# Summing two scattered halves in a fused decoder block: one half's loads ahead of the last tiles, additions on two engines, and a norm's short steps between them

## The chip, the cores and the metric

The kernel runs on one core of one Trainium2 chip. The metric is device time in microseconds (us) of one execution of the whole kernel, as a median of several runs. A profile is one execution taken by the hardware profiler; its clock starts at the start of the span, and all times of day below (such as 1405.73) are us on that clock. Engines: PE (TensorE), DVE (VectorE), ACT (ScalarE), POOL (GpSimd), SP (SyncE, which here only issues DMAs).

## The reference

A post-norm decoder block on 4 x 512 tokens of width 512, in float32: causal self-attention with 16 heads and rotary embedding, cross-attention over a masked context of 1601 rows, and a mixture of 16 experts (top 4 of each token) plus a shared expert. Only the end matters here:

```python
def step(acc, ws):
    wg, wu, wd, cw = ws
    return (acc + cw[:, None] * _swiglu_ffn(x, wg, wu, wd), None)
routed, _ = lax.scan(step, jnp.zeros_like(x), (w_gate, w_up, w_down, combine.T))
shared = _swiglu_ffn(x, sw_gate, sw_up, sw_down)
...
x = _layernorm(x + _L0_ffn_ref(x, ...), axis=-1)
```

Each token's result is its input plus the shared expert's output plus four weighted expert outputs, and of that sum a layer norm without scale or bias is taken.

## The kernel before

The 2048 tokens lie in SBUF as `rows`, 128 partitions x NT = 16 token tiles x D = 512. The routed experts (`routed_experts`) work on TILES = 79 slot tiles, numbered m = 0 to 78, each of 128 rows that belong to one expert. For each tile POOL gathers the rows by an indirect DMA (`gather`, L1881), PE turns and multiplies them with the expert's weights in three passes, ACT weighs the output into `y` (`weigh_y`, L1934), and POOL sends it out by an indirect DMA that adds each row to its token's row in DRAM (`scatter`, L1890). Two such accumulators exist, `acc[0]` and `acc[1]` (in the profile both are `acc_rows`): tile m adds to `acc[m % 2]`, and since two scatters to one tensor may not overlap, scatter m waits until scatter m - 2 has landed. `acc[0]` starts out as the input plus the shared expert. The semaphores `y_added[0]` and `y_added[1]` count the landings.

SP loads the experts' weights (L1860, 3 MB each); after the last of them it waits at L1873 until both accumulators are complete, that is until tiles 77 and 78 have landed.

Then `finish_rows` runs. The 16 token tiles are taken in five parts, `PARTS = ((0, 2), (2, 6), (6, 10), (10, 14), (14, 16))`, called part 0 to part 4 here. SP issues ten loads (L2086), for each part the even half into `rows` and the odd half into `odd_rows`; parts of four tiles are 1 MB a half, the others 0.5 MB. A part's semaphore `row_in[k]` reaches 32 when both halves are in. DVE then does, part by part: the additions `rows + odd_rows` (L2105), the statistics (L677), their aggregation (L684), and the short steps of `normalise`: `half_v` (L696), reciprocal (L699) of the square root which ACT has taken meanwhile (`root`, L690), two products (L702), `rstd` (L704), and the shift (L709). With `by_scalar=True` ACT scales the part's rows (L721). ACT's own order is for each part: sqrt, wait for the shift, scale; so the next part's sqrt stands behind this part's scaling. SP stores a part (L2091) when its rows are scaled. POOL has nothing to do in this stage. The program order of each engine is the order written in the code; there is no scheduler.

Of the kernel before, what the change touches and what calls it, by code (L numbers as in the profile page):

```python
# [28 lines left out]
ALU = mybir.AluOpType  # L29
# [8 lines left out]
EPS = 1e-5  # L38
# [3 lines left out]
NT = B * TT  # L42
# [13 lines left out]
TILES = (NT * P * TOPK + E * (SLOTS - 1)) // SLOTS  # L56
# [604 lines left out]
def layer_norm(nc, sem, ctx, rows, name, by_scalar=False, parts=tuple((b * TT, b * TT + TT) for b in range(B))):  # L661
# [9 lines left out]
    eps_set, gathered, aggregated = sem(name + "_eps_set"), sem(name + "_gathered"), sem(name + "_aggregated")  # L671
# [7 lines left out]
    def aggregate(dve, b):  # L679
        if b == 0:  # L680
            nc.vector.memset(eps[:, :], EPS).then_inc(eps_set, 1)
        for t in range(*parts[b]):
            dve.wait_ge(gathered, t + 1)
            nc.vector.bn_aggr(mean_var[:, t, :], stats[:, t, :]).then_inc(aggregated, 1)  # L684

    def root(act, b):
        mine = slice(*parts[b])
        act.wait_ge(eps_set, 1)
        act.wait_ge(aggregated, parts[b][1])
        nc.scalar.activation(rstd[:, mine], mean_var[:, mine, 1], ACT.Sqrt, bias=eps[:, 0:1]).then_inc(rooted, 1)  # L690

    def normalise(dve, b):

        mine = slice(*parts[b])
        dve.wait_ge(aggregated, parts[b][1])
# [1103 lines left out]
def routed_experts(nc, block, sem, w_split, x2_rows, acc, plan, done, ends):  # L1799
# [7 lines left out]
    with ExitStack() as ctx:  # L1807
# [31 lines left out]

        def added(m):  # L1840

            return y_added[m % 2], 16 * (m // 2 + 1)
# [11 lines left out]
        def _(sp):  # L1854
# [17 lines left out]
            for par in range(2):  # L1872
                sp.wait_ge(y_added[par], 16 * ((TILES + 1 - par) // 2))  # L1873

        @block.gpsimd
        def _(pool):
# [9 lines left out]
            def scatter(m):  # L1886
                if m >= 2:
                    pool.wait_ge(*added(m - 2))
                pool.wait_ge(y_done, m + 1)
                nc.gpsimd.indirect_dma_start(  # L1890
                    acc[m % 2], bass.IndirectOffsetOnAxis(ap=token_row[:, 1, m:m + 1], axis=0),
                    y[:, m % YB, :], None, compute_op=ALU.add
                ).then_inc(y_added[m % 2], 16)
# [174 lines left out]


def finish_rows(nc, block, sem, rows, acc, out):  # L2070
# [4 lines left out]
    with ExitStack() as ctx:  # L2075
# [4 lines left out]
        summed, stored = sem("f_summed"), sem("f_stored")  # L2080
# [18 lines left out]

        @block.vector  # L2100
        def _(dve):
            for k, (first, last) in enumerate(PARTS):
                dve.wait_ge(row_in[k], 32)
                for t in range(first, last):
                    nc.vector.tensor_tensor(rows[:, t, :], rows[:, t, :], odd_rows[:, t, :], ALU.add  # L2105
                                            ).then_inc(summed, 1)
                for t in range(first, last):
                    dve.wait_ge(summed, t + 1)
                    gather(t)
                aggregate(dve, k)  # L2110
                normalise(dve, k)


def experts(nc, sem, rows, x2_norm, w_experts, w_split, gate_wT, expert_bias, out, ident):


    with ExitStack() as ctx:
# [14 lines left out]
        routed_experts(nc, block, sem, w_split, x2_rows, acc, plan, done, ends)  # L2132
        finish_rows(nc, block, sem, rows, acc, out)
# [71 lines left out]
```

## Time and profile before

| what | us |
|---|---|
| timed runs, median of 3 (lowest to highest) | 1449.95 (1443.52 to 1451.45) |
| the profiled execution | 1446.43 |
| its span | 1444.7 |
| last scatter starts | 1400.93 |
| first load of the last stage is issued | 1405.73 |
| DVE's first addition of part 0, of part 1 | 1410.46, 1416.30 |
| ACT's last row tile ends | 1441.47 |

PE is busy for 90% of the span, and the last stage of some 45 us is the part without it. To read it, take the chain of waits backwards from the end, then the timelines of POOL, SP, DVE and ACT for that stretch, and for each DMA the time from its issue to its landing.

### The profile page before, as it was taken

To read this page: it belongs to the slowest core of one execution; us is meant where nothing else is said; L and a number is where in the kernel's file an instruction comes from. 1 tells how busy PE (TensorE), PEld (TensorE's weight loads), DVE (VectorE), ACT (ScalarE), POOL (GpSimd) and SP (SyncE) were. 2 spreads that over 40 slices of the span, in tenths; PEclk is the share of its full clock that TensorE was granted. 3 is DMA by queue.
4 is the path that set the end of the run, shared out by engine and by line. 5 is a ranking of instruction groups with operands and counts; after the bars stand their busy time and mean duration, and the time that the engine had idled before them with its cause. 6 is when DMAs were issued, how large, how long until landed. Compare 5 with 4: busy or idle time off the path is not lost. (4 is left out here: it accounts for less than half of the span.)

```text
span 1444.7 us, 22221 instructions
## 1 busy us (share of the span) xinstructions
PE 1301.5 (90%) x7473; PEld 1034.2 (72%) x7473; DVE 837.1 (58%) x1770; ACT 710.3 (49%) x1590; POOL 378.7 (26%) x487
## 2 busy tenths in 40 slices
PE   5899999999999758999999997989999999899970
PEld 4666776767666447888888886777888887788850
DVE  6777677677767466675767656693333333233327
ACT  4788578578857624453544533313333333333324
POOL 0234223234222310000101000101554554465530
PEclk9999999999999879999999998999999999999995
DMA  5311211211110045577777574336979998986548
GB/s 189 117 52 45 74 62 70 73 46 58 68 45 1 1 151 187 197 262 261 245 244 247 203 261 172 150 121 223 289 194 326 234 257 272 280 217 116 108 70 333
DMA packets 91067, 235.59 MB, mean 163 GB/s; under 512 B 10632, under 2 KB 47500, under 8 KB 86224
## 3 DMA queue, kind: packets, MB, share of 16 engines
q1 hardware_dynamic: 73120, 188.96, 36.6%
q0 software_dynamic: 17840, 45.22, 15.0%
q8 instruction: 65, 1.06, 0.3%
q14 instruction: 42, 0.34, 0.1%
HBM read 146.20 MB, written 87.95 MB: 162 GB/s over the span
## 5 line engine op out<-in xcount | busy, mean ns | idle before, releaser
L2024 PE MATMUL e_both_ps<-e_w,e_x_t 128*128 x948 | 240.6, 402 | 0.0
L2024 PEld LDWEIGHTS e_both_ps<-e_w,e_x_t 128*128 128x128 f32 x948 | 172.5, 189 | 35.9
L513 PE MATMUL proj_ps<-wqkv,x_sp 128*128 128x384 f32 x768 | 172.4, 354 | 10.7 <-DVE wqkv L381 10.6
L1890 POOL DMA_INDIRECT acc_rows<-e_y,token_row x79 | 125.1, 1584 | 171.6 <-DMA acc_rows<-e_y,token_row 96.2
L1203 PE MATMUL c_score_ps<-ct,x_t 128*128 128x402 f32 x768 | 159.7, 362 | 0.0
L1226 PE MATMUL c_out_ps<-cr,weigh_t 128*128 128x512 f32 (+1 forms) x624 | 149.9, 397 | 1.4 <-DVE weigh_t L1033 1.4
L1203 PEld LDWEIGHTS c_score_ps<-ct,x_t 128*128 128x128 f32 x768 | 142.0, 196 | 5.6 <-issue 4.3
L264 POOL TENSOR_SCALAR_AFFINE_SELECT p_t<-p_t 128x128 f32<-128x128 f32 x256 | 87.3, 353 | 219.3 <-ACT p_t L358 215.4
L1959 DVE TENSOR_TENSOR e_x_t<-e_turn_ps,e_x_t 128x512 fp32r<-128x512 f32 x79 | 54.6, 692 | 152.0 <-ACT e_x_t L1921 152.0
L513 PEld LDWEIGHTS proj_ps<-wqkv,x_sp 128*128 128x128 f32 x768 | 130.8, 193 | 12.4 <-issue 11.0
L1226 PEld LDWEIGHTS c_out_ps<-cr,weigh_t 128*128 128x128 f32 (+1 forms) x624 | 115.8, 188 | 28.8 <-issue 1.7
L2047 PE MATMUL e_down_ps<-e_w,e_h_t 128*128 x474 | 126.4, 403 | 8.5 <-DVE e_h_t L1971 8.4
L358 ACT ACTIVATE p_t<-score_ps 128x512 f32<-128x512 f32 (+3 forms) x256 | 101.5, 436 | 47.2 <-PE score_ps L569 44.2
L2047 PEld LDWEIGHTS e_down_ps<-e_w,e_h_t 128*128 128x128 f32 x474 | 90.2, 191 | 31.8 <-issue 10.4
L1927 ACT ACTIVATE e_gated<-e_both_ps 128x256 f32<-128x256 f32 x79 | 30.4, 384 | 151.2 <-PE e_both_ps L2024 151.2
L1934 ACT ACTIVATE e_y<-e_down_ps,e_weight 128x512 f32<-128x512 f32 x79 | 54.3, 687 | 100.8 <-PE e_down_ps L2047 80.2
L334 ACT ACTIVATE score_ps<-score_ps,neg_row_max 128x128 f32<-128x128 f32 (+3 forms) x176 | 86.7, 493 | 28.7 <-DVE neg_row_max L459 27.9
L459 DVE TENSOR_REDUCE neg_row_max<-score_ps 128x1 f32<-128x128 f32 (+3 forms) x176 | 82.9, 483 | 28.9 <-PE score_ps L555 27.3
L569 PE MATMUL score_ps<-q_st,k_st 128*128 128x256 f32 (+2 forms) x256 | 86.0, 395 | 13.7 <-ACT p_t L358 12.7
L1966 DVE TENSOR_TENSOR e_h_f<-e_both_ps,e_gated 128x256 f32<-128x256 f32 x79 | 33.5, 425 | 108.2 <-ACT e_gated L1927 108.2
L1881 POOL DMA_INDIRECT e_x_g<-x_rows,token_row x79 | 77.3, 979 | 68.5 <-DVE token_row L1611 24.9
L569 PEld LDWEIGHTS score_ps<-q_st,k_st 128*128 128x128 f32 x256 | 42.6, 191 | 72.9 <-ACT p_t L358 53.6
(232 smaller groups left out, 2255.2 us busy)
## 6 DMA issues: line engine op xcount, KB each, us to landing
e_w<-w_split SPq DMA_DIRECT2D x15, 3072.0 KB, 12.9
w_split<-c_piece SPq DMA_DIRECT2D x96, 384.0 KB, 3.9
c_piece<-w_experts SPq DMA_DIRECT2D x96, 192.0 KB, 4.1
raw<-ctxT SPq DMA_DIRECT2D x16, 800.5 KB, 4.3
w_split<-rows SPq DMA_DIRECT2D x24, 512.0 KB, 3.4
raw<-ctx_rows SPq DMA_DIRECT2D x16, 768.0 KB, 4.8
acc_rows<-rows SPq DMA_DIRECT2D x8, 1024.0 KB, 8.5
rows<-w_experts SPq DMA_DIRECT2D x24, 256.0 KB, 2.6
```

Of the source, the lines that this page charges most:

```text
L264: nc.gpsimd.affine_select(out=block_of, in_=block_of, compare_op=ALU.is_ge, fill=0.0, base=0, pattern=[[1, P]], channel_multiplier=-1).the ...
L334: nc.scalar.activation(row_place(n)[:, 0:w], row_place(n)[:, 0:w], ACT.Exp, bias=neg_row_max[:, qt, h:h + 1], accum_out=row_sum[:, qt, h:h ...
L358: nc.scalar.activation(p_t[:, h, p_at[kc]:p_at[kc] + w], score_ps[:, n % 2, kc * P:T], ACT.Exp).then_inc(exped, 1)
L459: nc.vector.tensor_reduce(neg_row_max[:, qt, h:h + 1], row_place(n)[:, 0:(qt + 1) * P], AX, ALU.max, negate=True).then_inc(maxed, 1)
L513: mm = nc.tensor.matmul(proj_ps[:, tt, 0:GW], x_sp[:, xs, c, tt * P:(tt + 1) * P], wqkv[:, ws, c, hg * GW:(hg + 1) * GW], start=(c == 0 an ...
L569: nc.tensor.matmul(score_ps[:, n % 2, q0:T], k_st[:, h, kc * P:(kc + 1) * P], q_st[:, h, q0:T], start=True, stop=True).then_inc(scored_t, 1)
L1203: mm = nc.tensor.matmul(score_ps[:, f, 0:MQ], x1_t[:, xs, c, n % XR * P:(n % XR + 1) * P], ct[:, cs, c, f * MQ:(f + 1) * MQ], start=(late ...
L1226: mm = nc.tensor.matmul(out_ps[:, n % 2, :], weigh_t[0:k, ws, c, :], cr[0:k, cs, c, :], start=(c == 0 and m == 0), stop=(c == MC - 1 and m ...
L1881: nc.gpsimd.indirect_dma_start(x_g[:, m % XG, :], None, x2_rows, bass.IndirectOffsetOnAxis(ap=token_row[:, 0, m:m + 1], axis=0)).then_inc( ...
L1890: nc.gpsimd.indirect_dma_start(acc[m % 2], bass.IndirectOffsetOnAxis(ap=token_row[:, 1, m:m + 1], axis=0), y[:, m % YB, :], None, compute_ ...
L2024: mm = nc.tensor.matmul(both_ps[:, m % 2, :], x_t[:, m % 2, xs, c * P:(c + 1) * P], weights(slot, ws, c * GU, (c + 1) * GU), start=(c == 0 ...
L2047: mm = nc.tensor.matmul(down_ps[:, m % 2, :], h_t[:, m % 2, hs, i * P:(i + 1) * P], weights(slot, ws, DOWN + i * D, DOWN + (i + 1) * D), s ...
```

## The change

Three things are changed in the last stage.

1. Tile 78, the last, adds to `acc[1]` instead of `acc[0]`. So `acc[0]` is complete with tile 76, and scatter 78 waits for scatter 77. SP no longer waits at L1873; it waits for `acc[0]` alone, issues the five even loads, waits for `acc[1]`, and issues the five odd loads.
2. POOL does the additions of the second half of each part from part 1 on (tiles 4, 5, 8, 9, 12, 13 and 15; 7 of 16), DVE those of the others. DVE still takes the statistics of all tiles.
3. The short steps of `normalise` for part k - 1 are no longer taken at the end of part k - 1. They stand in part k's stretch, with DVE's own additions and statistics of part k one by one between them. The last part's follow at the end.

The eps memset of every norm counts on the semaphore of the aggregation instead of one of its own. The norms of the earlier stages call `normalise` without steps between.

```diff
-    def normalise(dve, b):
+    def normalise(dve, b, behind=lambda step: None):
...
         nc.vector.tensor_scalar(half_v[:, mine], mean_var[:, mine, 1], EPS, -0.5, ALU.add, ALU.mult
                                 ).then_inc(inverted, 1)
+        behind(0)
         dve.wait_ge(rooted, b + 1)
         nc.vector.reciprocal(rstd[:, mine], rstd[:, mine]).then_inc(inverted, 1)
+        behind(1)
         for n in range(2):
             dve.wait_ge(inverted, b * 5 + 2 + n)
             nc.vector.tensor_tensor(half_v[:, mine], half_v[:, mine], rstd[:, mine], ALU.mult).then_inc(inverted, 1)
+            behind(2 + n)
...
+        behind(4)
         dve.wait_ge(inverted, b * 5 + 5)
...
+        def acc_of(m):
+
+            return 1 if m == TILES - 1 else m % 2
+
         def added(m):
 
-            return y_added[m % 2], 16 * (m // 2 + 1)
+            return y_added[acc_of(m)], 16 * (m // 2 + 1)
...
-            for par in range(2):
-                sp.wait_ge(y_added[par], 16 * ((TILES + 1 - par) // 2))
...
                 if m >= 2:
-                    pool.wait_ge(*added(m - 2))
+                    pool.wait_ge(*added(m - 1 if m == TILES - 1 else m - 2))
...
-                    acc[m % 2], bass.IndirectOffsetOnAxis(ap=token_row[:, 1, m:m + 1], axis=0),
+                    acc[acc_of(m)], bass.IndirectOffsetOnAxis(ap=token_row[:, 1, m:m + 1], axis=0),
...
+        return added(TILES - 3), added(TILES - 1)
...
-            for k, (first, last) in enumerate(PARTS):
-                for dst, src in ((rows, acc[0]), (odd_rows, acc[1])):
+            for dst, src, whole in ((rows, acc[0], sums[0]), (odd_rows, acc[1], sums[1])):
+                sp.wait_ge(*whole)
+                for k, (first, last) in enumerate(PARTS):
                     sp.dma_start(dst[:, first:last, :],
...
+        def by_pool(k):
+
+            first, last = PARTS[k]
+            return range(last - (last - first) // 2, last) if k else range(0)
+
+        def add_up(engine, t, done):
+            engine.tensor_tensor(rows[:, t, :], rows[:, t, :], odd_rows[:, t, :], ALU.add).then_inc(done, 1)
+
+        @block.gpsimd
+        def _(pool):
+            for k in range(len(PARTS)):
+                if by_pool(k):
+                    pool.wait_ge(row_in[k], 32)
+                for t in by_pool(k):
+                    add_up(nc.gpsimd, t, summed_pool)
...
             for k, (first, last) in enumerate(PARTS):
+                own = [t for t in range(first, last) if t in own_tiles]
+
+                def behind(step):
+                    if step < len(own):
+                        sum_up(own[step])
+                    elif step < 2 * len(own):
+                        stats(own[step - len(own)])
+
                 dve.wait_ge(row_in[k], 32)
...
+                if k:
+                    normalise(dve, k - 1, behind)
+                else:
+                    for step in range(2 * len(own)):
+                        behind(step)
+                for t in by_pool(k):
+                    stats(t)
                 aggregate(dve, k)
-                normalise(dve, k)
+            normalise(dve, len(PARTS) - 1)
```

## Rows read from the trace of the kernel before

**Rows 1.** The page's head: span and number of instructions.
```profile
span 1444.7 us, 22221 instructions
```
**Rows 2.** The chain that ended last, from 1396: start us, us, what.
```profile
1400.93 4.60 DMA acc_rows<-e_y,token_row
...
1405.73 0.33 SPq L2086
...
1407.05 9.22 DMA odd_rows<-acc_rows
...
1416.30 2.50 DVE rows L2105 x4
...
1439.95 0.81 ACT rows L721
```
**Rows 3.** Timeline of POOL: start us, us, engine, line, operation [idle before <-releaser].
```profile
1393.27 1.55 POOL L1890 DMA_INDIRECT acc_rows<-e_y,token_row  x1 [3.31 <-ACT e_y L1934]
1397.68 1.55 POOL L1890 DMA_INDIRECT acc_rows<-e_y,token_row  x1 [2.86 <-ACT e_y L1934]
```
**Rows 4.** Line L1890 from 1370 on: issue to landing of the last eight scatters.
```profile
DMA to landing us min/median/max: 4.4/4.6/5.1
```
**Rows 5.** DMA issues: first to third of the ten, and the fifth; last column landing.
```profile
rows<-acc_rows SPq DMA_DIRECT2D x1, 512.0 KB, 3.4
odd_rows<-acc_rows SPq DMA_DIRECT2D x1, 512.0 KB, 4.3
rows<-acc_rows SPq DMA_DIRECT2D x1, 1024.0 KB, 7.2
...
rows<-acc_rows SPq DMA_DIRECT2D x1, 1024.0 KB, 11.2
```
**Rows 6.** DMA queues in 1411:1421, in 1236:1241 (two rows), in 1399.8:1402.2: packets, MB, share.
```profile
q1 hardware_dynamic: 582, 4.24, 101.0%
...
q1 hardware_dynamic: 69, 1.70, 87.8%
q0 software_dynamic: 64, 0.13, 14.6%
...
q0 software_dynamic: 144, 0.26, 81.2%
```
**Rows 7.** POOL's timeline beside a weight load, and the first scatter's issue to landing.
```profile
1230.94 1.59 POOL L1890 DMA_INDIRECT acc_rows<-e_y,token_row  x1 [8.23 <-DMA acc_rows<-e_y,token_row]
...
1243.74 1.59 POOL L1890 DMA_INDIRECT acc_rows<-e_y,token_row  x1 [6.76 <-DMA acc_rows<-e_y,token_row]
...
acc_rows<-e_y,token_row POOLq DMA_INDIRECT x1, 12.5
```
**Rows 8.** Timeline of DVE and POOL, 22 to 28 us.
```profile
22.46 0.69 DVE L401 TENSOR_TENSOR qk_cos<-qk_cos,qk_sin 128x512 f32<-128x512 f32 x1
...
24.33 1.26 POOL L253 TENSOR_TENSOR qk_sp<-qk_cos,qk_sp 128x512 fp32r<-128x512 f32 x1 [22.05 <-ACT qk_sp L304]
24.39 1.75 DVE L401 TENSOR_TENSOR qk_cos<-qk_cos,qk_sin 128x512 f32<-128x512 f32 x1
```
**Rows 9.** Timeline of the last stage, DVE and ACT.
```profile
1413.25 1.28 ACT L690 ACT_TABLE_LOAD   x1 [13.06 <-DVE norm_mean_var L684]
...
1418.71 2.46 DVE L677 BATCH_NORM_STATS2 norm_stats<-rows 128x6 f32<-128x512 f32 x4
...
1421.88 0.18 DVE L699 RECIPROCAL norm_rstd<-norm_rstd 128x4 f32<-128x4 f32 x1 [0.22 <-ACT norm_rstd L690]
1422.10 0.36 DVE L702 TENSOR_TENSOR norm_half_v<-norm_half_v,norm_rstd 128x4 f32<-128x4 f32 x2
...
1428.35 0.18 DVE L699 RECIPROCAL norm_rstd<-norm_rstd 128x4 f32<-128x4 f32 x1 [0.22 <-ACT norm_rstd L690]
...
1435.82 2.93 ACT L721 ACTIVATE rows<-rows,norm_half_v,norm_rstd 128x512 f32<-128x512 f32 x4 [1.04 <-DVE norm_half_v L709]
...
1438.66 0.28 ACT L690 ACTIVATE norm_rstd<-norm_mean_var,norm_eps 128x2 f32<-128x2 f32 x1
1438.97 0.17 DVE L699 RECIPROCAL norm_rstd<-norm_rstd 128x2 f32<-128x2 f32 x1 [0.36 <-ACT norm_rstd L690]
```

More of the change, by code:

```diff
@@ L680, in aggregate @@
         if b == 0:
-            nc.vector.memset(eps[:, :], EPS).then_inc(eps_set, 1)
+            nc.vector.memset(eps[:, :], EPS).then_inc(aggregated, 1)
         for t in range(*parts[b]):
@@ L1838, in routed_experts @@
         weighed = sem("e_weighed")
+        def acc_of(m):
+            return 1 if m == TILES - 1 else m % 2
         def added(m):
-            return y_added[m % 2], 16 * (m // 2 + 1)
+            return y_added[acc_of(m)], 16 * (m // 2 + 1)
+        assert TILES % 2 == 1
         def gathered(m):
@@ L2067, in _, with finish_rows @@
             back(TILES - 1, before)
-def finish_rows(nc, block, sem, rows, acc, out):
+        return added(TILES - 3), added(TILES - 1)
+def finish_rows(nc, block, sem, rows, acc, sums, out):
     PARTS = ((0, 2), (2, 6), (6, 10), (10, 14), (14, 16))
@@ L2098, in _, with sum_up, stats @@
                 root(act, k)
+        def by_pool(k):
[10 more added lines that the diff above has]
+                    add_up(nc.gpsimd, t, summed_pool)
         @block.vector
         def _(dve):
-            for k, (first, last) in enumerate(PARTS):
-                dve.wait_ge(row_in[k], 32)
[L2104 to L2109, printed above, removed]
+            def sum_up(t):
+                add_up(nc.vector, t, summed)
+            def stats(t):
+                if t in own_tiles:
+                    dve.wait_ge(summed, own_tiles.index(t) + 1)
+                else:
+                    dve.wait_ge(summed_pool, pool_tiles.index(t) + 1)
+                gather(t)
+            pool_tiles = [t for k in range(len(PARTS)) for t in by_pool(k)]
+            own_tiles = [t for t in range(NT) if t not in pool_tiles]
+            for k, (first, last) in enumerate(PARTS):
+                own = [t for t in range(first, last) if t in own_tiles]
[4 more added lines that the diff above has]
+                        stats(own[step - len(own)])
+                dve.wait_ge(row_in[k], 32)
+                if k:
+                    normalise(dve, k - 1, behind)
+                else:
+                    for step in range(2 * len(own)):
+                        behind(step)
+                for t in by_pool(k):
+                    stats(t)
                 aggregate(dve, k)
-                normalise(dve, k)
+            normalise(dve, len(PARTS) - 1)
 def experts(nc, sem, rows, x2_norm, w_experts, w_split, gate_wT, expert_bias, out, ident):
@@ L2131, in experts @@
         ends = route(nc, block, sem, rows, x2_norm, gate_wT, expert_bias, w_experts, x2_rows, acc, plan, done)
-        routed_experts(nc, block, sem, w_split, x2_rows, acc, plan, done, ends)
-        finish_rows(nc, block, sem, rows, acc, out)
+        sums = routed_experts(nc, block, sem, w_split, x2_rows, acc, plan, done, ends)
+        finish_rows(nc, block, sem, rows, acc, sums, out)
 def decoder_block(nc, xT, x, ctxT, ctx_rows, mask, wqkvT, woT, rope, w_experts, gate_wT, expert_bias, out):
```

11 lines of the change are left out of this document (5 added, 6 removed).

## The prediction, made before the changed kernel was built

> **What bounds the kernel now.** Read the page's head first: 1444.7 us of span [rows 1], and the profiled execution took 1446.43 us, so 1.73 us lie around the span. The three timed runs have a median of 1449.95, 3.5 us above that execution. Then read the chain of waits over the last 45 us, because every edit lies there [rows 2]. It says: the scatter of tile 78 goes out at 1400.93 and is 4.60 us on the chain; SP issues ten loads from 1405.73 on; VectorE starts on part 1 (token tiles 2 to 5) at 1416.30, when the loads of part 1 have landed; from there VectorE and ScalarE alternate until ScalarE's last pair ends at 1441.47 (1439.95 plus 1.52), and a store and the end take 3.2 us more. So two things can be saved: arrival of part 1, and time from there to 1441.47. I put the seam at the reciprocal of part 1, 1421.88 [rows 9].
>
> **The even sums' loads, moved ahead.** Tile 76 is now the last one in acc[0]. Its scatter starts at 1393.27 [rows 3] and lands 4.6 us later (the median of the last eight [rows 4]), so SP, which waits for nothing else by then, issues the five even loads from 1398.1 on, 7.6 us earlier than now. The first 1 MB of the present loads landed 4.7 us after the first issue (odd part 0: issued about 0.4 later, 4.3 to landing), 2 MB 8.1 us after it, 4 MB 13.0 us after it (7.2 and 11.2 to landing [rows 5]; these are the third and the fifth issue, 0.9 and 1.8 us after the first, since three issues lie between 1405.73 and 1407.05 [rows 2]). Alone, the even 4 MB would be in at 1411.
>
> **What they collide with.** Scatter 77 starts at 1397.68 [rows 3], so its packets run beside these loads; and scatter 78, which now must follow 77 on the same tensor, waits for its landing. Alone, a scatter lands in 4.6 us [rows 4], its 144 packets taking 81.2% of 2.4 us of 16 engines, or 0.22 us each [rows 6]. Part 1's and later loads come in packets of 8 KB, for a partition's four tiles in one run (4.24 MB make 518 of them, the other 64 of the 582 being the small ones that signal): 101.0% of 10 us of 16 engines, 0.31 us a packet [rows 6]. Where packets of 24 KB stood against a scatter (1.70 MB in 69 packets [rows 6]), it landed after 12.5 us, 7.9 more than alone [rows 7]. I scale that by packet size: a third of it, 2.6 us, beside 8 KB packets; scatter 77 meets 4 KB packets of part 0 for half of its time, so 1.3 us. Bounds: nothing, and the whole 7.9 us. Scatter 77 lands at 1397.68 + 4.6 + 1.3 = 1403.6. POOL starts the next one 0.3 us after a landing (1230.94 plus 12.5, then 1243.74) [rows 7]: 1403.9, which is 3 us later than 1400.93. It lands 7.2 us later, at 1411.1, and SP issues the odd loads at 1411.3 (the 0.2 us of now: 1405.53 to 1405.73 [rows 2]). The odd loads are not helped by the early start of the even ones alone: they go out 5.6 us later than the first load now.
>
> Odd part 0 then lands 3.4 us after its issue [rows 5], 1414.7, where now it is 1410.4. Part 1 is in with 1.5 MB; between 4.7 (1 MB) and 8.1 us (2 MB) I take 6.4: **1417.7, against 1416.3 now, 1.4 us later**. Half the loads are gone from the queue, but the queue begins that much later.
>
> The Trainium skill, page "DMA: Bandwidth & Descriptors", section "Queues, rings and completion order", says that each engine round-robins between queue rows at packet granularity. That is the mechanism of the scaling above. The trace agrees so far as 64 scatter packets passed beside 69 of the loads in 5 us [rows 6]; the sum goes by the 12.5 us of the row alone.
>
> **The additions on GpSimd.** VectorE loses 7 of 16 additions, each 0.6 us (2.50 us for four [rows 2]), 4.2 us in all. GpSimd's own take 1.26 us each [rows 8], seven of them about 9 us, and it begins each part when VectorE does, so it takes parts 1 to 4 in one run from 1417.8 on. But the two engines do not run freely beside each other: at 24.33 GpSimd began a 128x512 operation with two inputs, and a VectorE addition begun at 24.39, also with two inputs in SBUF, took 1.75 us, where the same line took 0.69 us two microseconds before; it was held for 1.06 us, to within 0.2 us of GpSimd's end [rows 8]. Of what VectorE does once part 1 is in, two additions of part 1 and four short steps of part 0 (L702 twice, L704, L709) have two inputs in SBUF, and with one-input statistics between them each can be caught. Working them through in order, GpSimd taking the next turn whenever VectorE does a one-input step: each GpSimd operation holds them for up to 1.1 us, and the sum over these six steps is 5.3 us; 0.7 us of it covers the wait for ScalarE's table load that is there anyway, so 4.6 us on the path. Bounds: 0, if nothing is held, and 7 x 1.1 = 7.7. I take 4.6, since the one row that shows two such operations at once shows a full hold.
>
> The Trainium skill states this as a rule in "SBUF — State Buffer", section "Who interferes with whom": a VectorE instruction with two SBUF inputs contends with a GpSimd instruction that reads SBUF, and the second fully blocks. Row and rule agree in kind. By the rule's "whole instruction", 1.27 us instead of 1.1, the held time would be 0.9 us more. It speaks against this change.
>
> **Part 1 up to the seam.** From arrival: the short steps of part 0 among two additions and two statistics, 3.0 us (2 x 0.6 + 2 x 0.6 + six short ones at 0.1, L702 showing two dependent ones in 0.36 [rows 9]); 0.7 us of waiting, because part 0's sqrt has its 1.28 us table load [rows 9] and now comes just ahead; two more statistics 1.2 (2.46 for four); aggregation, first short step and one addition 1.3. That is 6.2, so 1423.9 unblocked and 1428.5 held, against 1421.88 now: **+2.0, or +6.6 held**.
>
> **From the seam to the end.** Now two turns take 6.47 us each (1421.88 to 1428.35 and again) [rows 9], and the whole stretch 19.6 us to 1441.47. In the new order VectorE's own work in a turn is 4.9 us. But another wait ends last: ScalarE does the four rows of a part (2.93 us) before the next part's sqrt [rows 9]. Reciprocal to the last short step of the same part is now 2.35 us instead of 0.8, since additions and statistics stand between; plus 0.1, 2.93 and 0.35 for scaling and sqrt, the turn is 5.75 us. So the two turns save 1.4 us. The third loses: its sqrt, now at 1438.66 right behind the scaling that began at 1435.82 [rows 9], waits for a scaling that begins 1.5 us after the reciprocal, so it is 4.75 us against 4.15; the last part's short steps and two rows stay at 2.5. In all 18.75 against 19.6: **-0.85 us**. Without that queue on ScalarE the stretch would be some 3 us shorter still.
>
> **The rest at nothing.** The eps memset counts on another semaphore and one wait of ScalarE goes: no transfer or engine is moved. SP's closing wait is replaced by the two new ones. SP's stores stand behind its waits as now, and the last one follows the last rows. GpSimd's additions stand behind scatter 78 on its queue, long landed by then.
>
> **Sum.** +6.6 - 0.85 = +5.75, less 0.25 us by which the same steps put in order overshoot the present timeline: **+5.5 us**. On the profiled execution 1446.4 + 5.5 = 1451.9; on the median 1455.5, which I give.
>
> **Rivals.**
> (1) *The engines do not hold each other*, or only for a tenth of it. Against it is the row at 24.39; for it, that it is one row. 2.0 - 0.85 - 0.25 = +0.9: 1450.9. Chance 0.15.
> (2) *The scatters are held behind the even loads until these are in.* For it: in rows 7 the scatter's 12.5 us reach past the whole load. Against: packets are a third of the size here. Then 77 lands at 1411 + 0.3, 78 starts at 1411.6 and lands at 1416.2, the odd loads go at 1416.4, 5.1 us later than forecast: +10.6, 1460.5, slower. It decides from a landing of scatter 78 at about 1413 on, where the loss passes 0.5%. Chance 0.15.
> (3) *Nothing stands in the way*: scatter 77 unharmed at 1402.3, 78 at 1402.6 and 1407.2, odd part 1 in at 1414.5 (behind the even bytes), nothing held, and ScalarE's queue not in the way: 1.8 + 0.85 + 3 = -5.7: 1444.3. It needs three mechanisms to be absent. Chance 0.07.
> The forecast itself 0.63, its own range 1452 to 1460 by half a scatter's delay and by a hold between 2.3 and 6.
>
> **Numbers.** 0.5% of the median is 7.2 us, about what a measurement of this kernel can tell from no change: below 1442.7 is faster, above 1457.2 slower. Slower: 0.13 of rival 2 and 0.13 of the forecast's upper side, 0.26. Faster: 0.03 of rival 3 and 0.01 for a low base. Same 0.70. The range runs from 1447 (rival 1 with the profiled execution's base) to 1462 (rival 2 and a little more).
>
> **What would show it.** Scatter 78 starting at 1403.9 instead of 1400.93 and landing after 6 to 8 us; first odd load at 1411.3; VectorE additions in part 1 of 1.2 to 1.8 us and short steps of up to 1.2 us; afterwards ScalarE without a gap between scaling and sqrt, and reciprocals 5.75 us apart. An odd load before 1409, or no long VectorE additions, proves the respective step wrong; a part 1 arrival after 1420 points at rival 2.

## The result, and the profile after

The changed kernel takes 1454.46 us (median of 8 runs, 1452.09 to 1459.4), the kernel before 1448.36 us (8 runs beside them, 1443.52 to 1451.96). The ratio is 1.0044, with a 95% interval of 1.0027 to 1.0062: slower by 6.1 us, within the 0.5% named above, though the interval reaches a little over it. The forecast was 1455.5.

The two profiled executions differ by more than the medians, 1454.1 against 1444.7 us of span [rows 1]. The head of the page after:

```profile
span 1454.1 us, 22210 instructions
```

So the first question is where two traces may be compared at all. Scatter 76, the first DMA that the change touches, starts at 1395.94 here and at 1393.27 before [rows 3]. These 2.7 us arose in stages that the change leaves alone: in the thirteen profiles of this study scatter 76 starts anywhere from 1389.09 to 1401.77, and at 1396.51 in a kernel whose instructions are those of the kernel before up to that point (the loads alone, below). From here on every time is therefore counted **from the start of scatter 76**, written +x, and the time from there to the end of the span is called the tail. It is 51.43 us before and 58.16 after: **6.73 us**, where the medians say 6.1. A turn is the time from one part's reciprocal to the next part's.

The chain that ended last, in the changed kernel (start us, us, what), beside [rows 2]:

```profile
1400.35 9.42 DMA acc_rows<-e_y,token_row
1409.77 0.27 issue
1410.04 5.64 DMA acc_rows<-e_y,token_row
1415.69 3.82 DMA odd_rows<-acc_rows
...
1419.54 1.29 DVE rows L2116 x2
...
1449.33 0.81 ACT rows L725
```

Before, one scatter of 4.60 us stood on the chain. Now two do, one behind the other, and the first took 9.42 us. SP's odd loads go out at 1415.69, +19.75. The even ones had gone out at 1400.56. The timelines of SP's queue and POOL (start us, us, engine, line, operation, count, idle before and what ended it):

```profile
1400.56 2.43 SPq L2096 DMA_DIRECT2D rows<-acc_rows  x5
1415.69 2.45 SPq L2096 DMA_DIRECT2D odd_rows<-acc_rows  x5
```
```profile
1395.94 1.55 POOL L1897 DMA_INDIRECT acc_rows<-e_y,token_row  x1 [3.31 <-ACT e_y L1941]
1400.35 1.55 POOL L1897 DMA_INDIRECT acc_rows<-e_y,token_row  x1 [2.86 <-ACT e_y L1941]
1410.04 1.57 POOL L1897 DMA_INDIRECT acc_rows<-e_y,token_row  x1 [8.14 <-DMA acc_rows<-e_y,token_row]
1422.08 9.54 POOL L2116 TENSOR_TENSOR rows<-rows,odd_rows 128x512 f32<-128x512 f32 x7 [10.47 <-DMA odd_rows<-acc_rows]
```

The last line is also the landing of part 1: GpSimd waits for nothing else, so part 1 is in at 1422.08, +26.14 (before 1416.30, +23.03), 6.4 us after the first odd load. From there its seven additions run without a gap. What VectorE does beside them:

```profile
1422.35 1.01 DVE L696 TENSOR_SCALAR norm_half_v<-norm_mean_var 128x2 f32<-128x2 f32 x1
1423.27 0.68 DVE L2116 TENSOR_TENSOR rows<-rows,odd_rows 128x512 f32<-128x512 f32 x1
1423.87 0.15 DVE L700 RECIPROCAL norm_rstd<-norm_rstd 128x2 f32<-128x2 f32 x1
1423.95 1.67 DVE L2116 TENSOR_TENSOR rows<-rows,odd_rows 128x512 f32<-128x512 f32 x1
1425.54 1.21 DVE L704 TENSOR_TENSOR norm_half_v<-norm_half_v,norm_rstd 128x2 f32<-128x2 f32 x1
...
1427.28 0.69 DVE L704 TENSOR_TENSOR norm_half_v<-norm_half_v,norm_rstd 128x2 f32<-128x2 f32 x1
...
1428.50 0.69 DVE L707 SCALAR_TENSOR_TENSOR norm_rstd<-norm_half_v,norm_rstd 128x2 f32<-128x2 f32 x1
1429.23 1.18 DVE L713 SCALAR_TENSOR_TENSOR norm_half_v<-norm_mean_var,norm_rstd 128x2 f32<-128x2 f32 x1
...
1432.67 0.17 DVE L700 RECIPROCAL norm_rstd<-norm_rstd 128x4 f32<-128x4 f32 x1
1432.76 0.66 DVE L2116 TENSOR_TENSOR rows<-rows,odd_rows 128x512 f32<-128x512 f32 x1
1433.34 0.15 DVE L704 TENSOR_TENSOR norm_half_v<-norm_half_v,norm_rstd 128x4 f32<-128x4 f32 x1
```

The last two lines, once GpSimd is done at 1431.6, show what these operations take alone: 0.66 and 0.15 us. Against that, the lines above are longer by 0.84 (L696, 0.17 alone), 1.01, 1.06, 0.54, 0.54 and 1.02 us: **5.0 us of holding**. The reciprocal of part 1, the seam, is at 1432.67, +36.73 (before +28.61 [rows 9]). Behind the seam, the scaling of ScalarE and VectorE's reciprocals take turns:

```profile
1402.88 1.28 ACT L689 ACT_TABLE_LOAD   x1
...
1435.06 2.93 ACT L725 ACTIVATE rows<-rows,norm_half_v,norm_rstd 128x512 f32<-128x512 f32 x4 [2.84 <-DVE norm_half_v L713]
1437.89 0.28 ACT L689 ACTIVATE norm_rstd<-norm_mean_var,norm_eps 128x4 f32<-128x4 f32 x1
```
```profile
1438.21 0.18 DVE L700 RECIPROCAL norm_rstd<-norm_rstd 128x4 f32<-128x4 f32 x1 [0.84 <-ACT norm_rstd L689]
...
1443.75 0.18 DVE L700 RECIPROCAL norm_rstd<-norm_rstd 128x4 f32<-128x4 f32 x1 [0.85 <-ACT norm_rstd L689]
...
1448.35 0.17 DVE L700 RECIPROCAL norm_rstd<-norm_rstd 128x2 f32<-128x2 f32 x1 [2.16 <-ACT norm_rstd L689]
```

VectorE now idles 0.84, 0.85 and 2.16 us ahead of its reciprocals, because the square root stands behind four scaled rows on ScalarE. Before, two of these waits were 0.22 and 0.36 us, but a turn was 6.47 [rows 9]; now it is 5.54. One line is at a new place: the table load stands at 1402.88, +6.94, and not behind part 0's aggregation (before 1413.25, +19.98 [rows 9]).

The tail's 6.73 us are made up so, each from the times above: part 1 in 3.11 later; from there to the seam 10.59 instead of 5.58, 5.01 more; from the seam to the end 21.43 instead of 22.82, 1.39 less.

### The profile page after: what moved, and what is told of

Same layout as the page of the kernel before. It is cut to its first block and busy times, and to the rows that moved or that the text cites. A ratio compares the mean times of both kernels' runs of the same rounds, so it can differ in the third digit from the quotient of the medians.

```text
span 1454.1 us, 22210 instructions
## 1 busy us (share of the span) xinstructions
PE 1301.6 (90%) x7473; PEld 1033.1 (71%) x7473; DVE 835.9 (57%) x1763; ACT 710.1 (49%) x1590; POOL 388.2 (27%) x494
## 3 DMA queue, kind: packets, MB, share of 16 engines
q8 instruction: 65, 1.06, 0.3%
```

## The experiments

The theory: (a) the early even loads delay scatter 77, and with it 78 and all odd loads; (b) GpSimd's additions hold VectorE's operations with two inputs in SBUF; (c) the new order of the short steps gives a little back, limited by ScalarE's queue. The rivals: the loss is made by one of them alone, or by something that none of them names. "Timed" is the ratio to the kernel before, of runs on the same chip; its interval is some 2 to 3 us to each side, so that effects of 1 or 2 us are read from the profiles and only the large ones from the ratio. A tail and its ratio agree to within 2.5 us in every kernel below. Apart from the loads alone and tile 78 alone, every kernel built for these experiments also has the constant's semaphore as in the change.

Each tail is that of one execution, and a part of it is chance. In the six kernels that load as before (before, GpSimd alone, steps alone, all but the loads, constant's wait alone, gated) part 1 is in at anything from +22.14 to +23.53, though no edit of theirs lies ahead of that: 1.4 us. The column "from there" leaves this out. It goes from part 1's landing, or from the first addition of part 1 where VectorE came to it later, to the end, and it repeats well: 28.31 to 28.47 in the four kernels with the old steps and all additions on VectorE, 30.44 and 30.47 in the two with the new steps and no additions on GpSimd.

| kernel | part 1 in or begun | from there | seam | tail, us | against 51.43 | timed |
|---|---|---|---|---|---|---|
| before | +23.03 | 28.40 | +28.61 | 51.43 | | |
| changed | +26.14 | 32.02 | +36.73 | 58.16 | +6.73 | 1.0044 [1.0027, 1.0062] |
| loads alone | +29.05 | 28.44 | +34.62 | 57.49 | +6.06 | 1.0037 [1.0025, 1.005] |
| GpSimd alone | +22.14 | 28.59 | +28.30 | 50.73 | -0.70 | 0.9997 [0.9986, 1.0009] |
| steps alone | +22.16 | 30.44 | +28.44 | 52.60 | +1.17 | 1.0015 [1.0002, 1.0029] |
| all but GpSimd | +26.27 | 30.47 | +32.55 | 56.74 | +5.31 | 1.0023 [1.0007, 1.004] |
| all but the loads | +22.48 | 31.54 | +30.47 | 54.02 | +2.59 | 1.0023 [1.001, 1.0037] |
| tile 78 alone | +24.61 | 28.47 | +30.19 | 53.08 | +1.65 | 1.0001 [0.9983, 1.002] |
| GpSimd writes only | +26.11 | 27.03 | +31.68 | 53.14 | +1.71 | 0.9999 [0.9981, 1.0017] |
| small packets | +26.23 | 32.08 | +36.83 | 58.31 | +6.88 | 1.0056 [1.0038, 1.0075] |
| constant's wait alone | +23.53 | 28.31 | +29.06 | 51.84 | +0.41 | |
| gated | +23.36 | 26.49 | +28.28 | 49.85 | -1.58 | 0.998 [0.9964, 0.9997] |
| two parts early | +21.44 | 26.51 | +26.36 | 47.95 | -3.48 | 0.9981 [0.9965, 0.9996] |

**The loads alone.** The kernel before, with tile 78's sums in the odd tensor and the even loads ahead.

```diff
...
-            for k, (first, last) in enumerate(PARTS):
-                for dst, src in ((rows, acc[0]), (odd_rows, acc[1])):
+            for dst, src, whole in ((rows, acc[0], sums[0]), (odd_rows, acc[1], sums[1])):
+                sp.wait_ge(*whole)
+                for k, (first, last) in enumerate(PARTS):
...
```

> Edit 1 alone on the kernel before: tile 78 adds to acc[1], the five even loads go out behind scatter 76, the five odd ones behind scatter 78; additions and norm as before. The measure is the tail, from the start of scatter 76 to the end of the span: 51.4 us before, 58.2 after. Theory (the loads alone lose time: scatter 77 is held by the even loads, 78 waits for it, and parts 0 and 1 then arrive 2.5 us apart, so that part 0's work with its table load is no longer covered): odd loads issued 19.8 us after scatter 76's start, VectorE's first addition at 23.6, part 1's additions not before 29, tail 57.5, time 1454.5. Rival (the loads cost nothing, the loss of the changed kernel is all GpSimd's): tail 49 to 52, time 1446 to 1449.

The tail is 57.49 us: nearly the whole loss from this one edit. Scatter 77 took 9.7 us and 78 started at +14.36 and took 5.7, as in the changed kernel. VectorE in this kernel:

```profile
1420.29 1.29 DVE L2110 TENSOR_TENSOR rows<-rows,odd_rows 128x512 f32<-128x512 f32 x2 [19.38 <-DMA odd_rows<-acc_rows]
...
1424.69 0.17 DVE L699 RECIPROCAL norm_rstd<-norm_rstd 128x2 f32<-128x2 f32 x1 [1.50 <-ACT norm_rstd L690]
...
1425.56 2.49 DVE L2110 TENSOR_TENSOR rows<-rows,odd_rows 128x512 f32<-128x512 f32 x4
```

Its additions of part 1 begin without waiting for any load, at +29.05: part 0's block, 5.3 us with its 1.50 us wait for the table load, now bounds, and part 1's loads are in before it ends. (In the changed kernel the two are 2.5 us apart, 1419.54 and 1422.08.) Before, that block lay in the gap of 5.8 us between the two arrivals. So the loads cost 6.1 us here: 3.1 for part 1's arrival, if it is that of the changed kernel, and the rest for cover that is gone.

**Tile 78 alone.** As the last, but all loads wait for both sums, in the old order: it separates the order of the scatters from their collision with loads.

```diff
-            return y_added[m % 2], 16 * (m // 2 + 1)
+            return y_added[acc_of(m)], 16 * (m // 2 + 1)
...
-                    pool.wait_ge(*added(m - 2))
+                    pool.wait_ge(*added(m - 1 if m == TILES - 1 else m - 2))
...
```

> The kernel before with tile 78 adding to acc[1], but all ten loads issued as before, after both accumulators are complete. It measures what the order of scatters 77 and 78 costs without any load beside them. Theory: scatter 77 lands after 4.6 us, 78 starts 0.3 us later and lands after 4.6, the first load goes out 14.1 us after scatter 76's start instead of 12.5; tail (from scatter 76's start to the span's end) 53.0 against 51.4, time 1.6 us over before. Rival (the wait is passed by then anyway): scatter 78 7.7 us after 76, tail 51.4.

```profile
1397.54 1.55 POOL L1892 DMA_INDIRECT acc_rows<-e_y,token_row  x1 [2.86 <-ACT e_y L1936]
1402.57 1.57 POOL L1892 DMA_INDIRECT acc_rows<-e_y,token_row  x1 [3.49 <-DMA acc_rows<-e_y,token_row]
```

Scatter 77 took 4.8 us and 78, at +9.45, 4.9: the wait alone costs 1.8 us of start and 1.65 us of tail. The other 4.65 us of scatter 78's later start (+14.10 in the changed kernel) come from loads that run beside scatter 77.

**Small packets.** The changed kernel with the even loads tile by tile, so that they come in packets of 2 KB and not of 8. It tests the scaling with packet size that the prediction used.

```diff
+            for k, (first, last) in enumerate(PARTS):
+                for t in range(first, last):
+                    sp.dma_start(rows[:, t:t + 1, :],
...
```

> The changed kernel with the even half loaded by 16 loads of one token tile each, so that its packets are 2 KB instead of 8 KB; the odd half as it is. The question is why scatter 77 took 9.4 us beside the even loads, where 5.9 were forecast. Theory A (what scatter 77 loses is one packet of the load for each of its own, as forecast): it lands after 5.3 us. Theory B (its first packets come about 3 us late whatever the packets' size, and only then do the queues take turns): 8 to 8.5 us. The changed kernel's 9.4 is with 8 KB packets. Tail: A 54 to 55, B 57.

```profile
1393.50 1.55 POOL L1897 DMA_INDIRECT acc_rows<-e_y,token_row  x1 [2.86 <-ACT e_y L1941]
1401.55 1.57 POOL L1897 DMA_INDIRECT acc_rows<-e_y,token_row  x1 [6.50 <-DMA acc_rows<-e_y,token_row]
```

Scatter 77 landed after 7.8 us (1401.55 less the 0.3 of issue). With the packets a quarter of the size, its delay beyond the 4.6 alone is 3.2 us instead of 4.8: it shrinks by a third, not by three quarters. The queues show what it consists of (DMA queues, packets, MB, share of 16 engines). In the changed kernel, the first line of 1402.5:1405.3, the other two of 1405.3:1409.5:

```profile
q1 hardware_dynamic: 194, 1.10, 99.3%
...
q1 hardware_dynamic: 163, 1.20, 71.0%
q0 software_dynamic: 144, 0.26, 34.2%
```

In the kernel with small packets, the first line of 1395.6:1396.8, the second of 1396.8:1400.8:

```profile
q1 hardware_dynamic: 198, 0.35, 91.4%
...
q0 software_dynamic: 144, 0.26, 41.7%
```

Alone, a scatter's packets start 2.1 us after it (1397.68 [rows 3], window 1399.8:1402.2 [rows 6]), which would be at 1402.5 in the one and at 1395.6 in the other. In the changed kernel not one of scatter 77's packets was sent for 2.8 us from there, while the loads had the engines for themselves; then all 144 went within 4.2 us, instead of 2.4, beside 163 of the loads. Late start 2.8 and slower passage 1.8 make 4.6 of the 4.8 us. With small packets the silence was 1.2 us and the passage 4.0: 1.2 and 1.6 make 2.8 of the 3.2. So the late start is there at both sizes and is the part that shrank, while the passage hardly changed. Theory B, 3 us of late start whatever the size, came near the landing but is wrong in this. Why the first packets come late, no run here tells; nor is packet size the only difference between the two, since SP issued 16 loads over 8.3 us here and five over 2.4 us there.

Scatter 78 of this kernel took 7.6 us, since the smaller packets stretched the even loads into its time, and started only 1.6 us sooner. Odd loads and tail did not gain.

**GpSimd alone.** Loads and order of steps of the kernel before.

```diff
...
+            return range(last - (last - first) // 2, last) if k else range(0)
...
+                for step in range(2 * len(own)):
+                    behind(step)
+                for t in by_pool(k):
+                    stats(t)
...
```

> Edit 2 alone: GpSimd adds 7 of 16 token tiles; loads and the place of the short steps as before. Theory (GpSimd's additions hold every two-input instruction of VectorE, in part 1 and after): VectorE additions of 1.6 to 1.7 us and short steps of up to 1.2 us; the 4.2 us of additions taken off VectorE are given back, tail 52.0 (before 51.4), time within 2 us of before. Rival (no hold): tail 48.1, time 1445.

```profile
1423.86 2.36 DVE L2117 TENSOR_TENSOR rows<-rows,odd_rows 128x512 f32<-128x512 f32 x2 [0.95 <-DMA odd_rows<-acc_rows]
...
1428.92 1.24 DVE L696 TENSOR_SCALAR norm_half_v<-norm_mean_var 128x4 f32<-128x4 f32 x1
...
1430.27 1.30 DVE L704 TENSOR_TENSOR norm_half_v<-norm_half_v,norm_rstd 128x4 f32<-128x4 f32 x2
```
```profile
1423.91 3.43 POOL L2117 TENSOR_TENSOR rows<-rows,odd_rows 128x512 f32<-128x512 f32 x2 [12.90 <-DMA odd_rows<-acc_rows]
1428.87 2.48 POOL L2117 TENSOR_TENSOR rows<-rows,odd_rows 128x512 f32<-128x512 f32 x2 [1.52 <-DMA odd_rows<-acc_rows]
```

The holding is there: 2.36 us for two additions that take 1.29, L696 1.24 instead of 0.17, L704 1.30 instead of 0.36. It works both ways: where VectorE's addition began first, at 1423.86, GpSimd's pair took 3.43 us instead of 2.48. The tail is 0.7 us shorter than before and not 0.6 longer, but part 1 happened to be in 0.9 us sooner. From there to the end it is 28.59 us against 28.40: the seven additions taken off VectorE just about pay for the holding, 0.2 us short of it where I had expected 0.6.

**The steps alone.** Loads as before, all additions on VectorE.

```diff
...
+                if k:
+                    normalise(dve, k - 1, behind)
+                    for step in range(5, 2 * len(own)):
+                        behind(step)
...
-                normalise(dve, k)
+            normalise(dve, len(PARTS) - 1)
```

> Edit 3 alone: all additions on VectorE, loads as before, the short steps of a part between the additions and statistics of the next one. Theory (ScalarE takes the next sqrt only behind the scaling, which now starts later, so its chain ends last): reciprocals of parts 1, 2 and 3 are 6.2 us apart instead of 6.47, the last one comes later against the one before it than 4.15 us; tail 52 to 53, time 1448 to 1450. Rival (the covered short steps are a gain): turns of 5.8 us, tail 49 to 50, time 1446.5.

```profile
1438.28 0.18 DVE L700 RECIPROCAL norm_rstd<-norm_rstd 128x4 f32<-128x4 f32 x1 [0.25 <-ACT norm_rstd L689]
1443.82 0.17 DVE L700 RECIPROCAL norm_rstd<-norm_rstd 128x2 f32<-128x2 f32 x1 [2.82 <-ACT norm_rstd L689]
```

A turn is 6.02 us instead of 6.47, but the last reciprocal waits 2.82 us for ScalarE, and the tail is 1.17 us longer, as expected; from part 1 on it is 2.0 us longer, since here too part 1 was in 0.9 us sooner. Moving the short steps behind the next part's additions delays each part's scaling, and the last part has nothing left to cover that.

**All but GpSimd, and all but the loads.** The changed kernel without one part each.

```diff
-            return range(last - (last - first) // 2, last) if k else range(0)
+            return range(0)
...
                     normalise(dve, k - 1, behind)
+                    for step in range(5, 2 * len(own)):
+                        behind(step)
```

> The changed kernel with all 16 additions on VectorE (GpSimd adds none; loads early, short steps between). Theory (GpSimd's additions cost more by holding VectorE than they take off it, because all 7 run in parts 0 and 1): no VectorE addition above 0.7 us, tail 55.9 against 58.2 of the changed kernel, time 1452. Rival (GpSimd's additions are a gain and all the loss lies in the loads): tail 60, time 1457.

```diff
...
-            for dst, src, whole in ((rows, acc[0], sums[0]), (odd_rows, acc[1], sums[1])):
-                sp.wait_ge(*whole)
-                for k, (first, last) in enumerate(PARTS):
+            sp.wait_ge(*sums[0])
+            sp.wait_ge(*sums[1])
+            for k, (first, last) in enumerate(PARTS):
+                for dst, src in ((rows, acc[0]), (odd_rows, acc[1])):
```

> The changed kernel with the loads and the last tiles' sums of the kernel before (all loads behind both scatters, part by part, odd sums ending with scatter 77): GpSimd's 7 additions at once and the steps between additions are left. Theory (VectorE is held back by GpSimd's additions, about 5 us before part 1's reciprocal, as with the early loads, and the shorter turns give back about 2 us at most): part 1's reciprocal at about 31.8 us after scatter 76's start (28.6 before), tail about 53.5 us (51.43 before, 58.16 for the changed kernel), time about 2 us over the kernel before. Rival (the changed kernel's loss comes from its loads alone and the rest is a gain, as adding the two single edits' measured tails, 50.7 and 52.6 against 51.4, would have it to within a microsecond of no change): tail 51 to 52 us.

Without GpSimd's additions no VectorE addition takes over 0.69 us, and the tail is 56.74: in the changed kernel they cost 1.4 us. With the old loads the tail is 54.02. VectorE there:

```profile
1417.19 1.78 DVE L2117 TENSOR_TENSOR rows<-rows,odd_rows 128x512 f32<-128x512 f32 x1
...
1427.16 1.23 DVE L707 SCALAR_TENSOR_TENSOR norm_rstd<-norm_half_v,norm_rstd 128x4 f32<-128x4 f32 x1
1428.42 1.18 DVE L713 SCALAR_TENSOR_TENSOR norm_half_v<-norm_mean_var,norm_rstd 128x4 f32<-128x4 f32 x1
```

These hold 1.12, 1.08 and 1.02 us; with 1.01 at a second addition (1.67 us) and 0.65 at an L696 (0.82) it is 4.9 in all; my forecast put them all ahead of the seam (+31.8), but part fell behind it, so the seam stands at +30.47. Together with the two single edits this says that the parts do not simply add. From part 1 on, GpSimd alone costs 0.2 and the steps alone 2.0 us; together they cost 3.1. Under the new steps GpSimd's additions cost 1.1 us with the old loads (31.54 against 30.44) and 1.55 with the early ones (32.02 against 30.47), under the old steps 0.2: the new order puts operations with two inputs where GpSimd is at work. And the loads' +6.1 with these +2.6 would make 8.7, where the changed kernel has 6.7: with the early loads the new order lets VectorE begin part 1's additions before part 0's short steps are done, at +26.2 and not at +29.05, which gives back the lost cover.

So the changed kernel's 6.73 us can be laid out edit by edit: 3.1 for part 1's landing (loads), 2.1 for the new steps (30.47 against 28.40), 1.55 for GpSimd's additions in that order.

**GpSimd writes only.** GpSimd does a memset of about the same length in place of each addition. This leaves the seven sums out, as the expectation says, and keeps every wait.

```diff
-                for t in by_pool(k):
-                    add_up(nc.gpsimd, t, summed_pool)
+                for n, t in enumerate(by_pool(k)):
+                    nc.gpsimd.memset(scratch[:, 2 * (k - 1) + n, :], 0.0).then_inc(summed_pool, 1)
```

> The changed kernel with GpSimd's seven additions replaced by seven memsets of 1280 columns of a scratch tile, each about as long as an addition (1.3 us); those seven token tiles are not summed, everything else stands. Theory (VectorE is held because GpSimd reads SBUF): no addition, L704, L707 or L713 of VectorE is longer than alone (0.7, 0.16), L696 may be; tail 53.0 against 58.2. Rival (any work of GpSimd holds VectorE, or the long steps have another cause, such as the loads landing in the same memory): the same long steps as in the changed kernel and a tail of 57 to 58.

```profile
1424.37 0.89 DVE L696 TENSOR_SCALAR norm_half_v<-norm_mean_var 128x2 f32<-128x2 f32 x1
...
1425.12 0.67 DVE L2117 TENSOR_TENSOR rows<-rows,odd_rows 128x512 f32<-128x512 f32 x1
1425.71 0.15 DVE L704 TENSOR_TENSOR norm_half_v<-norm_half_v,norm_rstd 128x2 f32<-128x2 f32 x1
```

Beside a GpSimd that only writes, the second addition takes 0.67 us and L704 0.15, as alone. L696, the step with one input, is recorded with 0.89 us instead of 0.17, and the addition behind it with 0.81, but nothing starts later for it: the addition starts 0.07 us after L696 and the second one 0.75 us after it (1424.44 and 1425.12, from 1424.37), as in the kernel without GpSimd's additions (1423.23 and 1423.91, from 1423.16). Beside GpSimd's addition the hold of L696 was real: there the addition behind it started 0.92 us after it (1423.27, from 1422.35). The tail falls from 58.16 to 53.14: the holding is worth **5.0 us** of it, the sum read from the lines above. The Trainium skill has this as a rule, page "SBUF — State Buffer", section "Who interferes with whom": a VectorE instruction with two SBUF inputs contends with a GpSimd instruction that reads SBUF, not with one that only writes it, while a `tensor_scalar` may be in a mode that takes both ports. The first half agrees with these rows. The second does so far as L696 alone is recorded as longer beside memsets; which mode it ran in, no row shows.

**The constant's wait alone.** The kernel before, with the constant under the root counted on the aggregation's semaphore.

```diff
...
-        act.wait_ge(eps_set, 1)
-        act.wait_ge(aggregated, parts[b][1])
+        act.wait_ge(aggregated, 1 + parts[b][1])
...
```

> The kernel before with one thing of the change: the constant under the root and the aggregation count on one semaphore, so that ScalarE has one wait ahead of its first square root and not two. Theory (ScalarE loads the root's table ahead of the last wait in front of the square root, and a wait of its own for the constant, met only at part 0's aggregation, held that load back): the table load stands right behind ScalarE's last product of tile 78, about 7 us after scatter 76's start and not 20, VectorE's wait of 1.5 us for part 0's root is gone, and the tail stays 51.4 us within 0.5, since part 1's arrival comes later than the 1.3 us saved. Rival (the table load went early in the changed kernel because of its other edits): the table load stays at about 20 us.

```profile
1407.81 1.28 ACT L689 ACT_TABLE_LOAD   x1
```
```profile
1421.79 0.17 DVE L698 RECIPROCAL norm_rstd<-norm_rstd 128x2 f32<-128x2 f32 x1 [0.16 <-ACT norm_rstd L689]
```

The table load is at +6.95 and VectorE's wait is 0.16 us, not 1.50. One wait fewer moved 1.3 us off part 0's path; the tail, 51.84, did not gain, because part 1's arrival ends later there. This is one execution, and its turns are 6.40 us instead of 6.47. This is the edit that the prediction costed at nothing: right for this kernel by itself, wrong in the changed one, where part 0's block has lost its cover.

**A version without the collisions.** GpSimd adds one tile of each part of four, only after VectorE has done its own additions of that part; loads, tile order and steps as before.

```diff
...
+            return range(last - 1, last) if last - first == 4 else range(0)
...
+                    pool.wait_ge(summed, PARTS[k][1] - len([t for j in range(k + 1) for t in by_pool(j)]))
...
```

> The kernel before with GpSimd adding one token tile of each part of four (tiles 5, 9, 13), begun only when VectorE has done its own three additions of the part, so that it runs beside statistics, which have one input; the eps memset on the aggregation's semaphore. Theory (only two-input steps are held): no VectorE step is longer than alone, the turn from reciprocal to reciprocal is 5.9 us instead of 6.47, tail 49.6 against 51.4, time 1.8 us under before. Rival (GpSimd beside statistics holds VectorE too): tail 51 to 53.

GpSimd's additions then run beside VectorE's statistics, which have one input: no VectorE operation is longer than alone, a turn is 5.80 us, the tail 49.85 (from part 1 on 26.49 against 28.40), and the time 0.998 of before, an interval that leaves 1 out.

**Two parts early.** The same, with the odd halves of parts 0 and 1 alone loaded early, under scatter 78.

```diff
...
+            sp.wait_ge(*sums[1])
+            for k in range(2):
+                load_half(k, odd_rows, acc[1])
+            sp.wait_ge(*sums[0])
+            for k in range(2):
+                load_half(k, rows, acc[0])
...
```

> The gated kernel (GpSimd adds one tile of each part of four, only once VectorE has done its own) with the odd halves of parts 0 and 1 alone, 3 MB, loaded as soon as the odd sums are complete, which is at scatter 77's landing; scatter 78 stays in the even sums. The even halves of parts 0 and 1 follow once scatter 78 is in, then the rest part by part. Theory (a scatter is held back only if its packets come up for sending while the loads already stream, as scatter 77 of the changed kernel, which landed after 9.4 us; scatter 78 is free to go within a microsecond of the early loads' issue, since both wait for the same stretch): scatter 78 lands within 1 us of what it takes alone (4.6 to 5.7 us), the even halves of parts 0 and 1 find the odd ones in or nearly so, part 1 is in some 2.5 us sooner than in the gated kernel, and the tail from scatter 76's start to the end is about 47.5 us (gated kernel 49.85, before 51.43). Rival (loads and a scatter at the same time always cost the scatter 3 us and more): scatter 78 takes 8 to 10 us, which eats the whole head start: tail 50 to 52 us.

```profile
1403.12 1.57 POOL L1897 DMA_INDIRECT acc_rows<-e_y,token_row  x1 [1.71 <-ACT e_y L1941]
```
```profile
1404.73 0.83 SPq L2095 DMA_DIRECT2D odd_rows<-acc_rows  x2
```
```profile
acc_rows<-e_y,token_row POOLq DMA_INDIRECT x1, 4.8
```

Scatter 78 landed 4.8 us after its issue although two loads went out 1.6 us after it: its packets were on their way before theirs. Part 1 is begun at +21.44, and the tail is 47.95, 1.9 us less than gated and 3.5 less than before. The timed ratio, 0.9981, does not show the further 1.9 us over the gated kernel; its interval is too wide to say whether they are there in every execution. From part 1 on the two kernels are alike (26.51 and 26.49), so the 1.9 us are all in when part 1 begins, and since +23.36 is late among the landings with the old loads, up to 1.2 us of them can be chance.

## Why the prediction was right

The time lies 1.0 us from the forecast, and the mechanisms are the forecast ones: an arrival that comes later, VectorE held ahead of the seam, a small gain behind it. That it came so near is in part luck. The base was 1449.95, the median of three runs, and the eight runs give 1448.36, 1.6 us less; the change itself was 5.5 us forecast, 6.1 in the medians and 6.73 in the profiles. By its own steps:

**The collision of scatter 77: the term that was mis-sized.** 5.9 us forecast, 9.4 measured. I scaled the 7.9 us of [rows 7] with the size of the load's packets. What that row does not show, and my scaling left out, is a late start: 2.8 us in which none of the scatter's packets go, and only then the alternation. The small-packet kernel shows that the delay as a whole does not go with packet size: 3.2 us where a quarter of 4.8 would be 1.2. My upper bound, the whole 7.9, held it.

**Scatter 78.** 7.2 us forecast, 5.6 measured, since it started 3.5 us later than forecast and most of the even loads were in by then (the last landed at about 1414.6). Its packets too began late, at 1413.4 where 1412.1 would be usual, and then passed in 2.0 us. The errors, 3.5 too little and 1.8 too much (0.2 of it SP's issue), leave the odd loads at +19.75 instead of +18.0. That the wait for 77 costs something by itself was forecast (3 us with the collision); alone it is 1.8.

**Part 1 in 6.4 us after the first odd load.** Measured 6.4 (1415.69 to 1422.08). So part 1 is in 3.1 us later than before, and not 1.4.

**The hold.** Six steps, 5.3 us forecast, 4.6 of it on the path; measured 5.0 at six operations, and 5.0 on the path (58.16 against 53.14). The six are not quite those forecast: the first addition went free, and L696, with one input, was held 0.84 us. That is a kind of operation that my reading of [rows 8] did not cover.

**Part 1 to the seam.** 6.2 unheld and 10.8 in all forecast, 10.59 measured, 5.6 of it unheld. The 0.7 us of waiting for the table load did not occur, because the load had moved ahead of the wait. "The rest at nothing" was thus wrong by 0.7 us, on the good side.

**From the seam to the end.** Turns of 5.75, 5.75 and 4.75 us forecast, 5.54, 5.54 and 4.60 measured; to ScalarE's last row 18.18 us instead of 18.75. I had added the whole root behind the scaling where the two overlap by 0.1 us, and 0.1 us twice ahead of it. VectorE's waits of 0.84 and 2.16 us show ScalarE's queue as the bound that was named.

**Sum.** Forecast +1.4, +5.2, -0.85 and -0.25 make +5.5. Measured +3.1, +5.0 and -1.4 make +6.7. The arrival was 1.7 us too good, the way to the seam 0.2 and the end 0.3 too bad, so half a microsecond of the miss was made good by others.

**The rivals.** Engines that do not hold each other (1450.9): the writes-only kernel and the held lines are against it. Scatters held until the loads are in (1460.5): scatter 77 landed at 1409.77, while the even loads still ran to about 1414.6; a delay of that kind exists, but it ended on its own. In size it came to that rival's edge: scatter 78 landed at +19.74, which is 1413.0 on the prediction's clock, the landing from which on the rival was to decide. Nothing in the way (1444.3): all three things were in the way. Its 5.7 us of gain were not reached either: the two-parts-early kernel, in which none of the three is in the way but which differs in other things too, has a tail 3.5 us shorter than before.

**What the forecast lacked** is an account of which part of the change costs what. I read the hold as the main loss (4.6 of 5.5). Taken singly, the loads cost 6.1 us, the new steps 2.0 and GpSimd's additions 0.2; within the changed kernel, taking GpSimd's additions out gains 1.4, since the additions they save VectorE are worth 3.6 of the 5.0 that they hold it.

## What to carry to other kernels

Before a load is moved ahead, ask which small transfer it will meet and who waits for that transfer; a scatter whose packets are not yet on their way when a stream of loads begins was 4.8 us late here, while one issued 1.6 us ahead of the loads was not late at all. Work given to GpSimd beside VectorE should be placed under VectorE operations with one input, by a wait if need be: seven additions that ran at once cost 5 us of holding, three that were gated cost none. And an arrival that spreads two parts also covers the work between them; when both arrive together, the first part's block is on the path even though nothing in it grew.

## What the runs showed that I had not expected

- A scatter on GpSimd's queue that met a running stream of loads had no packet sent for 2.8 us beyond its usual start, with 4 and 8 KB packets beside it, and for 1.2 us with 2 KB packets, where it was still 3.2 us late in all.
- The two engines hold each other down to the smallest operations: a 128x2 product of 0.15 us took 1.21 us beside a 128x512 addition on GpSimd, and GpSimd's own pair took 3.43 us instead of 2.48 where VectorE was first.
- A one-input VectorE operation (`tensor_scalar`, 128x2) was held too, 0.84 us beside additions, when reciprocals and statistics were not. Beside memsets its record was 0.72 us longer, but what followed it started as early as without them.
- ScalarE's table load ran 13 us earlier once its square root had one wait instead of two in front of it.
